# The x of batch b + 3 loaded into the dead q and k of attention 3, its scaling and adjacency product in queues of their own, and a new table of ranks

## What is computed

```
norm_adj = adj * dinv[:, None] * dinv[None, :]        # dinv = rsqrt(row sums)
x = layernorm(x + norm_adj @ (x @ W0) + b0)                                        # graph convolution
x = layernorm(x + attention1(x))        # 8 heads, masked by adj, projection, o + layernorm(o)
for 3 steps: a = adj @ h; z, r = sigmoid(..); c = tanh(a @ w5 + (r * h) @ u5); h = (1 - z) h + z c   # GRU
x = layernorm(x + h)
x = layernorm(x + attention3(x))        # 8 heads, masked by adj
```

## Time and profile before

| | |
|---|---|
| median of 3 runs | 2841.97 us (2840.41 to 3499.7) |
| profiled execution | 2836.56 us, of which the span of the trace is 2834.8 us |
| busy share of the span | PE 92%, DVE 87%, ACT 59%, POOL 52% |
| DMA queues | 20% of 16 engines, 47 GB/s on average |

### The profile page before, as it was taken

The page is one execution under the profiler, slowest core; times in us unless marked ns, Lnnn a source line. Parts: engine busy times, 40 slices in busy tenths (PEclk is TensorE's granted clock), DMA queues, the critical chain, the costliest instruction groups (busy, mean ns, idle before and its releaser), DMA issues.

```text
span 2834.8 us, 50080 instructions
## 1 busy us (share of the span) xinstructions
PE 2594.9 (92%) x16825; PEld 2007.0 (71%) x16825; DVE 2463.6 (87%) x5962; ACT 1686.0 (59%) x3559; POOL 1474.8 (52%) x1787
## 2 busy tenths in 40 slices
PE   7878989999999998989989899998989989898997
PEld 6556767777776776767777677777767777676775
DVE  7978889899898988989899898998988889889676
ACT  4434755748466574755747467474665746545677
POOL 2756456445745546565455654446555464657312
PEclk8889999999999999999999999999999999999999
DMA  5211202212031121202212031121301222021022
GB/s 142 45 26 23 59 18 61 50 38 59 20 77 31 38 59 47 65 18 50 59 40 59 18 68 42 39 59 34 69 26 37 59 53 59 18 48 36 12 46 68
DMA packets 93231, 132.80 MB, mean 47 GB/s; under 512 B 16977, under 2 KB 42226, under 8 KB 92978
## 3 DMA queue, kind: packets, MB, share of 16 engines
q1 hardware_dynamic: 92978, 129.60, 19.7%
HBM read 19.83 MB, written 8.39 MB: 10 GB/s over the span
## 4 chain that ended last, share of the span: by engine, by line
DVE 37%; PE 35%; POOL 15%; issue 9%; ACT 3%; SPq 1%; DMA 1%; POOLq 0%; DVEq 0%; ACTq 0%
DVE PT L1490 8%; PE bank L1728 7%; PE bank L1730 7%; PE bank L1729 7%; PE bank L1836 4%; POOL acc L1111 4%; POOL acc L1113 4%; PE bank L1782 3%; PE bank L1851 3%; DVE gate L1608 3%; POOL acc L1115 3%; DVE probs L1473 2%; DVE bank L1465 2%; DVE vh L1573 2%; DVE gate L1606 2%
## 5 line engine op out<-in xcount | busy, mean ns | idle before, releaser
L1490 DVE SCALAR_TENSOR_TENSOR PT<-adjT,PT 128x512 f32<-128x512 f32 x512 | 471.8, 969 | 49.3 <-ACT PT L1212 48.5
L1220 ACT ACTIVATE probs<-probs,few 128x512 f32<-128x512 f32 x512 | 367.5, 723 | 45.9 <-DVE few L1473 44.5
L1115 POOL TENSOR_TENSOR acc<-PT 128x256 f32<-128x256 f32 x256 | 240.3, 962 | 229.2 <-DVE PT L1490 219.1
L1465 DVE CUSTOM_DVE_ANT_0 bank<-bank,mask 128x512 f32<-128x512 f32 x512 | 344.7, 702 | 11.2 <-PE bank L1782 5.9
L1473 DVE CUSTOM_DVE_ANT_0 probs<-bank,mask 128x512 f32<-128x512 f32 x512 | 336.5, 684 | 15.1 <-PE bank L1836 9.3
L1212 ACT ACTIVATE PT<-bank 128x512 f32<-128x512 f32 x512 | 273.0, 599 | 119.6 <-PE bank L1805 103.9
L1836 PE MATMUL bank<-before_ident,probs 128*128 128x128 f32 x2048 | 302.2, 276 | 13.4 <-ACT probs L1220 5.5
L1782 PE MATMUL bank<-stack 96*128 96x512 f32 x768 | 282.7, 437 | 15.6 <-DMA stack<-qk 10.5
L1836 PEld LDWEIGHTS bank<-before_ident,probs 128*128 128x128 f32 x2048 | 236.0, 141 | 84.9 <-DVE few L1473 23.3
L1728 PE MATMUL bank<-feat,W 128*128 128x512 f32 x640 | 268.2, 419 | 7.8 <-DVE feat L1441 3.2
L1079 POOL TENSOR_TENSOR feat<-o,feat 128x256 fp32r<-128x256 f32 x128 | 101.7, 794 | 326.5 <-ACT feat L1249 326.5
(11 more groups left out here) (136 smaller groups left out, 6897.0 us busy)
## 6 DMA issues: line engine op xcount, KB each, us to landing
stack<-qk SPq DMA_DIRECT2D x576, 128.0 KB, 2.4
qk<-qk SPq DMA_DIRECT2D x192, 128.0 KB, 2.4
res<-in_x_dram SPq DMA_DIRECT2D x16, 512.0 KB, 3.8
out_dram<-res SPq DMA_DIRECT2D x16, 512.0 KB, 2.9
stack<-feat SPq DMA_DIRECT2D x192, 2.0 KB
rows<-bo_sum SPq DMA_DIRECT2D x15, 128.0 KB, 2.9
rows<-in_L_gnn_bias_dram SPq DMA_DIRECT2D x14, 128.0 KB, 3.0
rows<-in_L_gnn_ln_beta_dram SPq DMA_DIRECT2D x14, 128.0 KB, 3.0
```

The costliest lines, as they stand in the source:

```text
L1115: k = pool.tensor_tensor(to, first, second, ALU.add)
L1220: k = act.activation(p, p, ACT.Exp, bias=least[:, t % P_RING:t % P_RING + 1], scale=-1.0, accum_out=sums[:, later_at[grp] % 2, q * HG + h: ...
L1465: k = dve.tensor_tensor_reduce(out=place("scores", t)[:, :], in0=place("scores", t)[:, :], in1=mask1[:, q, :], scale=1.0, scalar=3.4e38, o ...
L1490: k = dve.scalar_tensor_tensor(p, adjT[:, HI, 2 * i:2 * i + 2, half * QH:(half + 1) * QH].bitcast(F32), 0.0, p, ALU.not_equal, ALU.min)
```

## The change

The load of batch b + 3 goes into the part of `qk` of its stream that holds the second half of k, high and low (`x_in`). It is issued as two DMAs as soon as the last copies of q and k of attention 3 of batch b into the buffer `stack` have landed, and no longer waits for the store of b. Scaling (ACT, DVE), the bias (POOL) and the residual in the first DVE step after W0 read `x_in` instead of `res`. Load, scaling, bias and the product with adj of batches 3 to 15 are put in queues `("front", ...)` of their own, so the planner may place them among the work of batch b. New waits: the scaling waits for the last minimum of head 0 of attention 3 of b; moving the ax product into `feat` waits for proj3 of b on PE; the step after W0 waits for the store of b; the statistics move to another place in `qk`, so proj3's addition waits for a minimum of head 1. All of RANK's 137 entries are replaced by others. UNITS, tile sizes and the arithmetic stay.

```diff
-RANK = {"act a": -1.06, "act c": 7.45, "act hT": 12.43, "act hf": 88.57, "act k": 1047.99, "act n1": 49.17,
+RANK = {"act a": -24.31, "act ax": 244.57, "act c": 10.79, "act hT": 4.43, "act hf": -1.18, "act k": 6.35,
...
-        if b >= STREAMS:
-            add(sp, "SP", ("load", b), ("store", b - STREAMS))
+        early = b >= STREAMS
+        pe_x, act_x, dve_x, pool_x, sp_x = (("front", *of) if early else of for of in (pe, act, dve, pool, sp))
+        if early:
+            add(sp_x, "SP", ("load", b), *[("stack", 3, b - STREAMS, 1, h) for h in range(HG)])
         for t in range(NT):
-            add(act, "ACT", ("act", "scale", b, t), ("load", b), ("prep", "DVE", "dinv"))
-            add(dve, "DVE", ("dve", "scale", b, t), ("act", "scale", b, t))
-        add(*((dve, "DVE") if b < STREAMS else (pool, "POOL")), added("scale", b), ("dve", "scale", b, NT - 1),
+            add(act_x, "ACT", ("act", "scale", b, t), ("load", b), ("prep", "DVE", "dinv"),
+                *([("stt", last_of_head(3, b - STREAMS, 1, 0))] if early else []))
+            add(dve_x, "DVE", ("dve", "scale", b, t), ("act", "scale", b, t))
+        add(*((pool_x, "POOL") if early else (dve, "DVE")), added("scale", b), ("dve", "scale", b, NT - 1),
             ("row", row_at["scale", b]))
         for f in range(FT):
-            add(pe, "PE", ("pe", "ax", b, f), ("dve", "scale", b, NT - 1), ("prep", "DVE", adjs[-1]), opens=[("ax", b, f)])
-            evacuated(b, ("ax", b), f)
+            add(pe_x, "PE", ("pe", "ax", b, f), ("dve", "scale", b, NT - 1), ("prep", "DVE", adjs[-1]), opens=[("ax", b, f)])
+            evacuated(b, ("ax", b), f, *([("pe", "proj3", b - STREAMS, NT // 2 - 1)] if early else []))
...
             add(dve, "DVE", ("dve", "w0", b, tp), ("pe", "w0", b, tp), added("scale", b),
-                frees=[("w0", b, tp)])
+                *([("store", b - STREAMS)] if early else []), frees=[("w0", b, tp)])
...
-                        sp.wait_ge(stored[b % STREAMS], b // STREAMS * 16)
-                    sp.dma_start(res[b % STREAMS][:, :, :], x_v[b]).then_inc(x_loaded[b % STREAMS], 16)
+                        for h in range(HG):
+                            at, loads = loads_of(3, b - STREAMS, 1, h)
+                            sp.wait_ge(stacked[at], loads)
+                        for i in range(2):
+                            sp.dma_start(x_in[b % STREAMS][:, i, :, :],
+                                         x_v[b][:, i * NT // 2:(i + 1) * NT // 2, :]).then_inc(x_loaded[b % STREAMS], 16)
...
-                k = act.activation(nat[j][:, HI, t, :], res[j][:, t, :], ACT.Copy, scale=dinv[:, t:t + 1])
+                k = act.activation(nat[j][:, HI, t, :], x_rows(b, t), ACT.Copy, scale=dinv[:, t:t + 1])
```

More of the change, by code:

```diff
@@ L331, in last_in_place, with last_of_head @@
         layer, b, g, h = mine[n - 1]
+        return ("exp" if layer == 1 else "stt"), last_of_head(layer, b, g, h)
+    def last_of_head(layer, b, g, h):
         after = (unit_at[layer, b, g] + 1) * SIDE
-        if layer == 1:
-            return ("exp", after - HG + h)
-        return ("stt", after - (HG - h) * QT + QT - 1)
+        return after - HG + h if layer == 1 else after - (HG - h) * QT + QT - 1
     def before_in_ring(t):
@@ L345, in adj_resnorm_kernel, with evacuated @@
     add = order.add
-    def evacuated(b, name, f):
-        add(("act", b % STREAMS), "ACT", ("act",) + name + (f,), ("pe",) + name + (f,),
+    def evacuated(b, name, f, *after):
+        add(("act", b % STREAMS), "ACT", ("act",) + name + (f,), ("pe",) + name + (f,), *after,
             *([("prep", "PE", "u3"), ("prep", "PE", "u5")] if name == ("ax", 2) else []))
@@ L673, in adj_resnorm_kernel @@
         ka = [qk[j][:, 1, :, :].rearrange("p s (f n) -> p s f n", f=FT) for j in js]
-        stats = [gate[j][:, 0, 0, 0:6 * NT].rearrange("p (t c) -> p t c", t=NT) for j in js]
+        x_in = [qk32[j][:, 1, :, N:2 * N].rearrange("p s (u d) -> p s u d", u=NT // 2) for j in js]
+        stats = [qk32[j][:, 1, 0, 0:6 * NT].rearrange("p (t c) -> p t c", t=NT) for j in js]
         at = nc.sbuf_base
@@ L709, in adj_resnorm_kernel, with x_rows @@
         deg = probs[:, 2, 0:3 * NT].rearrange("p (i t) -> p i t", i=3)
+        def x_rows(b, t):
+            return x_in[b % STREAMS][:, t // 2, t % 2, :] if b >= STREAMS else res[b % STREAMS][:, t, :]
         def wide(r, n):
@@ L968, in _ @@
                     if b >= STREAMS:
[L969 to L970 removed]
+                        for h in range(HG):
[4 more added lines that the diff above has]
+                                         x_v[b][:, i * NT // 2:(i + 1) * NT // 2, :]).then_inc(x_loaded[b % STREAMS], 16)
+                    else:
+                        sp.dma_start(res[b][:, :, :], x_v[b]).then_inc(x_loaded[b], 16)
                 elif key[0] == "store":
@@ L1089, in biases @@
                 pool.wait_ge(row_loaded, 16 * (row_at[what, b] + 1))
+                if what == "scale":
+                    i = pool.tensor_tensor(x_in[j], x_in[j], rows[:, 0:1, :].unsqueeze(1).broadcast_to([P, 2, NT // 2, D]), ALU.add)
+                    biased[j].raised_by(i, "b0")
+                    return
                 i = pool.tensor_tensor(res[j][:, :, :], res[j][:, :, :], wide(0, NT), ALU.add)
-                biased[j].raised_by(i, {"scale": "b0"}.get(what, what))
+                biased[j].raised_by(i, what)
             def feature_lo(b, s, f, src, step):
@@ L1189, in evacuate_hi @@
                 wait_full(act, *name)
+                if name[0] == "ax" and name[1] >= STREAMS:
+                    wait_full(act, "proj3", name[1] - STREAMS, NT // 2 - 1)
                 if name[:2] == ("ax", 2):
@@ L1555, in w0_norm @@
                     k = dve.scalar_tensor_tensor(res[j][:, t, :], place("w0", b, tp)[:, i * D:(i + 1) * D],
-                                                 dinv[:, t:t + 1], res[j][:, t, :], ALU.mult, ALU.add)
+                                                 dinv[:, t:t + 1], x_rows(b, t), ALU.mult, ALU.add)
                     summed[j].raised_by(k, f"n0{t}")
```

47 lines of the change are left out of this document (26 added, 21 removed), and 12 rows, old and new, of the table RANK.

## The result

| | before | after |
|---|---|---|
| median | 2841.19 us (4 runs, 2838.3 to 3499.7) | 2981.01 us (4 runs, 2975.6 to 2984.8) |
| span of the profiled execution | 2834.8 us | 2977.2 us |
| ratio | | 1.0494, 95% interval 1.0471 to 1.0518 |

The ratio leaves out the one slow execution of the kernel before, 3499.7 us. The changed kernel is 5% slower. I had forecast 2796 us, with 2745 to 2885 as the range and 0.14 for slower by over 2%.

What follows compares the result with a forecast made beforehand. No one engine bounds the kernel: PE sets attention 3 and the new batch, DVE holds PE in the turnover. Twelve periods saving 3.8 us give 46: 2836.6 - 46 = 2790.6, plus 5.4 to the median: 2796 us, range 2745 to 2885.

Steps and rivals of the forecast that it cites:

- The count of PE's work: Steady period: PE's work per stretch from matmul counts and warm pitches, 51.6, 68.8 and 39.5 us, sum 159.9.
- the DVE list of the new batch: New batch: DVE is the limit, its listed work taking 45 us, between 40 and 50.
- One period taken for twelve: Steady part: period falls from 170.8 to 167.0 us, 3.8 saved; twelve such periods save 46 us.
- Start and tail at zero: Start (to batch 3) and tail: left as they are, no time gained or lost.
- It removes 4.8 us of DVE per turnover, 62 us over 13: Turnover: four scalings (3.2 us) and L1608's stretch beside POOL (1.6 us) leave DVE.
- I cost the move at nothing: Attention 3: DVE's 2.95 us left there cover the scalings' 1.9 to 3.2; uncovered, up to 41 us.
- Load, SP, store: 13 more DMAs and SP's wait for the load cost nothing; the step after W0 waits about 3 us for the store.
- Cold clock: Some turnovers: matmuls after PE's wait start at the 1.2 GHz level, 2.3 us per twelve; nothing added to the sum.
- (d): New batch: DVE beside POOL slower, maskings at 1.44 us, stretch 57 us, period 179.0, 98 us lost: 2940 us; chance 0.15.
- (c): Turnover: PE's scaling wait turns into one for the GRU state or the store; nothing moves, 2842 us; chance 0.17.
- (b): All of the turnover's loss goes, DVE's new-batch stretch needing 40 us: put at 2765 us; chance 0.24.
- Signs: Right if: scaling wait gone, turnover about 70 us, PE idle in new batch ended by masking or sums, L1562 mostly 0.47 us.

Runs made afterwards that it cites:

- pinned kernels: Change's buffers and waits in the order of before, only load, scalings and b0 addition moved: 2830.5 us; same with scalings earlier and apart: 2816.5 us.
- POOL's cut on before: Kernel before with POOL's second and third addition of each tile's sums done for 16 of 256 columns: 2682.7 us, ratio 0.9450.
- before with one number moved: Kernel before with one number of its RANK table changed, pe r at -6.03 for -6.53: 3094.2 us, ratio 1.0911.
- the cut scalings: Kernel before with DVE's scalings of x from batch 3 on done for 16 of 256 columns, at their old place: 2828.5 us, ratio 0.9961.

## Why the prediction was wrong, step by step

**Period and place of the loss.** At the turnover to batch 12 I forecast 51.6 + 0.6, 68.8 and 46 us; measured are 49.1, 74.6 and 55.0. The count of PE's work was right: it is busy 160.8 us, where I had 159.9. The step that failed there is the DVE list of the new batch, put at 45 (40 to 50) "because the turnover has been relieved and will overlap the first of it". It took 55.0: 49.6 busy and 5.4 waiting. The 16 maskings took 11.7 us, 0.73 each, nearer to my low end (10.2) than to the high one (15.5); the minima took 7.7, the two states 5.5, and the rest 24.7 where I had some 20. And nothing overlapped. DVE idled 18.3 us in the turnover; I read that as waiting on PE. The turnover was 5.8 us over: 4.4 of PE idle, 4.2 of it for a GRU state that stands behind the step after W0, and 1.4 of PE being busy longer. I added up busy times of engines by stretch, which holds only if the order lets them lie beside each other.

**One period taken for twelve.** This step failed too, and it weighs more. The twelve periods are alike in the kernel before, and I took them to be alike with the change, so that the lists at batch 12 stood for all. The trace has three such periods. In the first eight the work is laid out otherwise: the new batch takes 68 to 83 us and not 46, with 300 to 461 matmuls where the one at batch 12 has 267, and DVE is busy over 61 us in it. The first long period has 65.2 us of turnover, 70.2 of new batch and 58.9 of attention 3, against 68.8, 46 and 52.2: the turnover was right there, and the new batch is 24 us over. Four periods of 191 to 195 us lose 87 us. I forecast 3.8 us saved per period; 9.0 are lost on average, and 7.9 in the one whose lists I had counted.

**Start and tail at zero.** Right for the start (3.5 us), wrong for the tail (31 us). My own condition (a move of over 15 us means a missing term) is met by the tail. I had the order's lists and looked at the steady part only.

**"It removes 4.8 us of DVE per turnover, 62 us over 13".** The removed work was real: the turnover is 4.0 us shorter in both pinned kernels, and L1562 has a median of 478 ns. But work off DVE isn't time. In its old place 17.8 us off DVE gave 11 us, since the GRU state was next in line. Of the 62 us the two pinned kernels kept 5 and 20.

**"I cost the move at nothing".** Wrong. DVE had 2.95 us free in attention 3, but at the end of it the minima are urgent. Attention 3 grew by 3.9 us with the scalings in one block behind ACT, and by 1.8 with them apart. The cover was a sum over 45 us; the wait was at one place.

**Load, SP, store.** Right as far as the traces show. No wait of DVE for the store is in them, and the pinned kernels, with the 13 more DMAs, are not slower than the one before.

**Cold clock "goes with the wait, nothing added".** Wrong in the changed kernel: the wait went elsewhere and was longer, and the clock followed. The mean granted clock of the new batch is 0.84. PE's busy time for the same matmuls goes with the clock in these four kernels: 2540.8 us at 0.985 (POOL's cut on before), 2594.9 at 0.967, 2653.1 at 0.932, 2687.8 at 0.922 (before with one number moved). By this 58 of the 142 us are time of PE at the lower clock; no run holds the clock and changes the order, so the split is read from the busy times and not shown.

**Rivals.** (d) gave 2940 us from a period of 179.0, at 0.15. The period at batch 12 came out at 178.7 and the stretch at 55 for 57, but that is luck: its mechanism wanted maskings of 1.44 us, and they took 0.73, and most of the loss arose in other periods. (c) had the sign right that PE's wait for the state would pass 60 us (69.3), and named the mechanism that the cut scalings show; it priced it at no change. (b) needed DVE's stretch at 40 us, and is out. What was missing is a rival in which the new order is poor as such. I took the new table as a rebalancing whose parts can be added up, and spread my chances around zero.

**Signs.** Of those that I had named for being right, the scaling wait is gone and PE's idle time sits in the new batch; most of it is ended there by the GRU state and none by maskings or sums. That the wait for the state passed 60 us was my sign of (c), and its price, no change, was wrong.

The Trainium skill ("SBUF — State Buffer", section "Who interferes with whom") was named for DVE beside POOL. POOL's instructions on 16 columns instead of 256 took the masking's mean from 969 to 790 ns in the kernel before, and DVE's busy time for the 512 maskings from 471.8 to 380.8 us. The minima of attention 1, with a single input in SBUF, stayed at 702 ns. Both agree with the rule. The page makes an exception for its two-port modes, which my sentence left out; no run here tests them.

## What to carry to other kernels

When a change comes with a new order, hold the order still first: move only the moved pieces in the old lists, and compare. The greedy planner turned half a unit in one tie-break into 6% of the time one way and 9% the other here, so two orders can't be compared by what their tables mean, and a gain of 1% in one part says nothing until the order is pinned or found anew for it.

Look at every period before one stands for all. The one that was counted here lost 8 us, and three others of the same run lost 22 to 24.

Read the waits of a stretch as a queue: who is late next. PE waited 21 us less for the scaling and 15 us more for the GRU state, another result of the same engine, due right after. And measure what a cut took off before judging what it gave: 16 columns of 256 left more than half of the time.

A moved instruction costs at its place, not on average. Put it behind its producer by more than the producer's own backlog (three tiles here), and look at what stands behind it in the same list.

## What I had not expected of the hardware

POOL's additions of 128 x 16 elements took 438 and 373 ns where those of 128 x 256 took 946 and 907: a sixteenth of the columns still takes over a third of a microsecond. The cut of over half of their time gave the kernel before 5.5%, though POOL is busy only 52% of its span. DVE's maskings are busy 91 us less, and PE's wait for the sums, 35.9 us before, falls to 0.3; how the 156 us divide between the two is not shown. These are the groups of the kernel before with the cut:

```profile
L1112 POOL TENSOR_TENSOR acc<-acc,PT 128x16 f32<-128x16 f32 x256 | 112.2, 438 | 7.6 <-DVE PT L1491 7.4 <-issue 0.2
...
L1114 POOL TENSOR_TENSOR acc<-acc,PT 128x16 f32<-128x16 f32 x256 | 95.4, 373 | 20.1
...
L1491 DVE SCALAR_TENSOR_TENSOR PT<-adjT,PT 128x512 f32<-128x512 f32 x512 | 380.8, 790 | 50.0 <-ACT PT L1213 49.2
```
